# A two-attention decoder kernel: key copies shared by VectorE and ScalarE, later waits in TensorE's scores, and the first weights of the second attention on a semaphore of their own

## The reference, cut to what matters

```python
# layer 0, 16 heads of 32
q, k, v = split(x @ q_out), split(x @ k_out), split(x @ v_out)
w = softmax(where(causal, -inf, q @ k.T / sqrt(32)))
y = concat(w @ v) @ w_out
# layer 1, the same after a low-rank projection
...
cq  = layernorm(x @ W_dq)  * q_ln_g  + q_ln_b      # 512 -> 128
ckv = layernorm(x @ W_dkv) * kv_ln_g + kv_ln_b     # 512 -> 128
q = cq @ W_uq;  k, v = split(ckv @ W_ukv)
```

## Time and profile before

| what | value |
|---|---|
| time, median of 3 runs | 3426.01 us (3419.97 to 3428.82) |
| profiled execution: its own time | 3417.81 us |
| profiled execution: span | 3415.9 us |
| mean granted clock of TensorE | 0.954 |
| PE busy | 2988.1 us (87%) |
| DVE busy | 1672.7 us (49%) |
| ACT busy | 1237.4 us (36%) |
| POOL busy | 630.5 us (18%) |
| stage a0 | from the start to about 430 us |
| stage a1 | about 1722 to 2143 us |

### The profile page before, as it was taken

The page is one execution under the profiler, slowest core; times in us unless marked ns, Lnnn a source line. Parts: engine busy times, 40 slices in busy tenths (PEclk is TensorE's granted clock), DMA queues, the critical chain, the costliest instruction groups (busy, mean ns, idle before and its releaser), DMA issues. The chain is left out here.

```text
span 3415.9 us, 47727 instructions
## 1 busy us (share of the span) xinstructions
PE 2988.1 (87%) x16274; PEld 2012.9 (59%) x16274; DVE 1672.7 (49%) x3192; ACT 1237.4 (36%) x3212; POOL 630.5 (18%) x703
## 2 busy tenths in 40 slices
PE   6999958888883999999968888699999999899998
PEld 4676623333331777777734554588888888644443
DVE  5666657667771311111136666466666666311222
ACT  2324316655563211111124434455565555211111
POOL 1000031223222000000010002233333333110332
PEclk9999979988996999999989999899999999999999
DMA  1000056776554100000010011111121110522342
GB/s 62 25 25 12 19 128 139 148 151 127 124 134 127 61 13 13 13 13 13 7 47 25 25 37 56 50 44 50 50 75 62 50 49 26 188 63 85 109 170 74
DMA packets 128570, 229.67 MB, mean 67 GB/s; under 512 B 17061, under 2 KB 33765, under 8 KB 128400
## 3 DMA queue, kind: packets, MB, share of 16 engines
q1 hardware_dynamic: 98352, 174.73, 18.7%
q0 software_dynamic: 14096, 32.50, 3.1%
q10 hardware_dynamic: 15952, 20.15, 1.8%
HBM read 167.68 MB, written 61.00 MB: 67 GB/s over the span
## 5 line engine op out<-in xcount | busy, mean ns | idle before, releaser
L1393 DVE TENSOR_REDUCE x_minus_max<-banks 128x2 f32<-128x1024 f32 x256 | 308.1, 1223 | 156.3 <-PE banks L1459 154.6
L1341 ACT ACTIVATE x_probs<-banks 128x512 f32<-128x512 f32 x512 | 272.1, 598 | 140.3 <-PE banks L1477 131.6
L570 ACT ACTIVATE a_probs<-banks,a_minus_max 128x128 f32<-128x128 f32 (+1 forms) x512 | 209.1, 427 | 143.1 <-DVE a_minus_max L656 141.9
L2222 POOL TENSOR_TENSOR x_probs<-x_probs,x_inverse 128x512 f32<-128x512 f32 x128 | 133.3, 1042 | 266.5 <-DVE x_inverse L2428 266.5
L1477 PEld LDWEIGHTS banks<-x_stacked_q,x_stacked_k 53*128 53x128 f32 x512 | 62.1, 195 | 202.3 <-issue 155.0
L1477 PE MATMUL banks<-x_stacked_q,x_stacked_k 53*128 53x512 f32 x512 | 155.9, 514 | 27.6 <-ACT x_probs L1341 20.6
L2286 ACT ACTIVATE x_probs<-banks,x_minus_max,x_rroot 128x256 f32<-128x256 f32 x256 | 143.1, 567 | 87.9 <-DVE x_minus_max L2394 87.9
L3057 PE MATMUL banks<-m_w,m_xT 128*128 x368 | 169.0, 603 | 4.6 <-issue 4.6
L1459 PE MATMUL banks<-x_stacked_k,x_stacked_q 51*128 51x512 f32 x512 | 135.3, 478 | 42.7 <-DVE x_whole L1410 13.2
L656 DVE TENSOR_REDUCE a_minus_max<-banks 128x2 f32<-128x512 f32 (+1 forms) x192 | 131.7, 686 | 77.7 <-PE banks L810 59.7
L1809 DVE TENSOR_TENSOR f_hT<-banks,f_silu 128x256 f32<-128x256 f32 (+1 forms) x88 | 37.2, 424 | 265.6 <-ACT f_silu L1722 265.6
(11 more groups left out here) (385 smaller groups left out, 7739.6 us busy)
## 6 DMA issues: line engine op xcount, KB each, us to landing
x_parts_dram<-x_parts SPq DMA_DIRECT2D x16, 1024.0 KB, 6.0
x_x<-x_after SPq DMA_DIRECT2D x24, 512.0 KB, 4.2
x_stacked_k<-x_parts_dram SPq DMA_DIRECT2D x96, 128.0 KB
x_stacked_q<-x_parts_dram SPq DMA_DIRECT2D x96, 128.0 KB
x_after<-a_z SPq DMA_DIRECT2D x16, 512.0 KB, 2.7
x_z<-x_after SPq DMA_DIRECT2D x16, 512.0 KB, 6.6
x_heads_dram<-x_heads_out SPq DMA_DIRECT2D x32, 256.0 KB, 3.7
x_after<-x_z SPq DMA_DIRECT2D x16, 512.0 KB, 3.3
```

The costliest lines, as they stand in the source:

```text
L570: ins = act.activation(probs[:, n % 3, i * width:(i + 1) * width], psum[uses.bank(use)][:, i * width:(i + 1) * width], ACT.Exp, bias=minus ...
L1341: act.activation(probs[:, n % 8, :], psum[at.bank(f"exp{n}")], ACT.Exp, scale=SCALE)\
L1393: dve.tensor_reduce(minus_max[:, c % 2, h % 4:h % 4 + 2, t], at.pair(use), AX.X, ALU.max, negate=True)\
L2222: pool.tensor_tensor(probs[:, s % 4], probs[:, s % 4], inverse[:, s, :].unsqueeze(2).broadcast_to([P, TT, S1]), ALU.mult)\
```

## The change

Four edits, all in `self_attention`:

1. The four copies of k1 move from DVE's program to ACT's, behind q0 and q1 and ahead of v0 and v1. DVE keeps those of k0.
2. Ahead of S0, PE waits for q0, q1 and k0 alone. It waits for k1 ahead of S6, and for v0 and v1 ahead of the first `context`.
3. The two loads of w_down are issued by ACT, ahead of w_o, and count a new semaphore, `down_loaded`. PE waits for it ahead of the low-rank product.
4. PE's wait for the other small loads (six now) moves from its start to the head of each sequence.

```diff
-        SMALL = 8
+        down_loaded = sem("down_loaded")
+        SMALL = 6
 ...
         def _(pool):
             if latent:
-                pool.dma_start(w_down[:, :, 0:RANK], weights["dq"].rearrange("(c p) n -> p c n", p=P)).then_inc(weights_loaded, 16)
-                pool.dma_start(w_down[:, :, RANK:], weights["dkv"].rearrange("(c p) n -> p c n", p=P)).then_inc(weights_loaded, 16)
 ...
         def _(act):
+            if latent:
+                act.dma_start(w_down[:, :, 0:RANK], weights["dq"].rearrange("(c p) n -> p c n", p=P)).then_inc(down_loaded, 16)
+                act.dma_start(w_down[:, :, RANK:], weights["dkv"].rearrange("(c p) n -> p c n", p=P)).then_inc(down_loaded, 16)
 ...
+                act.wait_ge(k_cleared, 1)
+                use = f"k1.{u}"
+                wait_full(act, use, turn)
+                for i in range(4):
+                    rows = slice(DH * i, DH * i + DH)
+                    ins = act.copy(k_of_head[rows, 8 + i:8 + i + 5:4, :],
+                                   psum[uses.bank(use)][rows, :].rearrange("p (c t) -> p c t", c=2))
+                ins.then_inc(free[uses.bank(use)], 1)
                 for j in range(TT):
                     use = f"v{j}.{u}"
 ...
                 dve.wait_ge(k_cleared, 1)
-                for j in range(2):
-                    use = f"k{j}.{u}"
+                use = f"k0.{u}"
 ...
         def _(pe):
-            if latent:
-                pe.wait_ge(weights_loaded, 16 * SMALL)
 ...
             def low_product(turn, u, own):
+                pe.wait_ge(down_loaded, 32)
 ...
             def sequence(turn, u, following):
                 if latent:
                     wait_bank(pe, f"v1.{u}", turn)
+                    pe.wait_ge(weights_loaded, 16 * SMALL)
 ...
                     if n == 0:
-                        for w in ("q0", "q1", "k0", "k1", "v0", "v1"):
+                        for w in ("q0", "q1", "k0"):
                             wait_free(pe, f"{w}.{u}", turn)
+                    if n == 6:
+                        wait_free(pe, f"k1.{u}", turn)
 ...
+                    if c == 0:
+                        for w in ("v0", "v1"):
+                            wait_free(pe, f"{w}.{u}", turn)
```

More of the change, by code:

```diff
@@ L642, in sequence @@
                 dve.wait_ge(k_cleared, 1)
-                for j in range(2):
-                    use = f"k{j}.{u}"
[L645 to L650, removed]
+                use = f"k0.{u}"
+                wait_full(dve, use, turn)
+                for i in range(4):
+                    rows = slice(DH * i, DH * i + DH)
+                    ins = dve.tensor_copy(k_of_head[rows, i:i + 5:4, :],
+                                          psum[uses.bank(use)][rows, :].rearrange("p (c t) -> p c t", c=2))
+                ins.then_inc(free[uses.bank(use)], 1)
                 def row_max(n):
```

## The result

| | before | changed |
|---|---|---|
| median of the runs | 3425.28 us (3419.97 to 3428.82, 4 runs) | 3376.17 us (3368.01 to 3380.50, 4 runs) |
| profiled execution, its span | 3417.81, 3415.9 | 3374.49, 3372.7 |

The ratio is 0.9857, with a 95% interval of 0.984 to 0.9874: 49 us or 1.4% less. Forecast were 3381 us and 44.6 us less.

What follows compares the result with a forecast made beforehand. PE, 87% busy, was taken as the bound, so gains come from its idle or slow time: 7.3 + 22.5 + 8.5 + 6.3 = 44.6 us off the 3426.01 median gives 3381.4 us; range 3370 to 3400.

Steps and rivals of the forecast that it cites:

- The likeliest case: Whole kernel: all gains in a0 and a1 arrive, 44.6 us less, median 3381.4 us; chance 0.53.
- VectorE copies only k0: a1, ahead of S0: four fewer copies let S0 start 2.8 us earlier in each of eight sequences, 22.5 us.
- the clock: a1, S0 to S3: five slow sequences become fast with shorter idleness, 5 x 1.70 = 8.5 us; lower bound 0.
- The head: Start of a1: transposes start when x lands, not after the last small load; 6.3 us, or 2.2.
- ScalarE's copies: a1 and a0, four k1 copies at 0.48 us each on ScalarE: nothing waits, price 0.
- a0: a0, ahead of S0: the wait for v0 and v1 goes, 7.3 us over eight sequences; lower bound 6.1.
- The clock gives nothing: a1: the half clock moves to another stretch of the sequence, so 8.5 us are lost, 3390 us; chance 0.22.
- The head is held by DMA: Start of a1: x lands after 10.2 us, sharing engines with w_down; 4.1 us lost, 3385.5 us; chance 0.12.
- Copies dear: a1: ScalarE's copies take 1.4 us each, so a1's sequences gain only 10.4 us; 3402 us; chance 0.06.
- slower: a1: ScalarE's copies take 2.5 us each and delay the first exponential, 25 us lost; 3437 us; chance 0.03.
- Nothing in a1: a1: S0 meets another wait as late as the old; only a0 and head gain, 3412 us; chance 0.04.

Runs made afterwards that it cites:

- e1: Kernel before, with k1 copied by ScalarE ahead of v0 and v1, S0 still waiting for all six; 3412.86 us, ratio 0.997.
- e2: Kernel before, with only the shorter waits (S0 for q0, q1, k0); VectorE still copies both k; 3396.14 us, ratio 0.9932.
- e3: Kernel before, with only w_down on ScalarE's queue with its own semaphore and other small loads waited for later; 3416.66 us, ratio 0.9977.
- e9: Changed kernel, with k0 projected ahead of q0 and q1 in each sequence; 3364.27 us in one run.
- e6: Changed kernel, with four more ScalarE copies of k1 into an unread tile ahead of the bank's release; 3388.77 us, ratio 0.9896.
- e4: Changed kernel, with w_down issued by GpSimd ahead of the other small loads, still on its own semaphore; 3385.30 us, ratio 0.9896.
- e7: Kernel before, with k1 copied by ScalarE plus four unread copies, S0 still waiting for v1, now later; 3424.55 us in one run.
- e8: Changed kernel, with w_down laid out as 4 KB rows and loaded by one DMA; 3371.33 us in one run.
- e5: Changed kernel, with w_o issued only behind the first x^T copies, w_down left on ScalarE; 3380.77 us, ratio 0.9877.
- e10: Changed kernel, with both w_down in one 4 KB-row transfer and k0 projected first; 3368.47 us, ratio 0.9854.

## Why the prediction was right

**The sum, term by term.** The likeliest case came in, at 3376 against 3381. In a1 the profile gives 37.2 us, and the steps gave 22.5 + 8.5 + 6.3 = 37.3. The mechanism is the one forecast; that the numbers meet to 0.1 us is partly luck, since terms that were too large and too small cancel. Ahead of the first S0 a1 gained 10.3 us (39.1 to 28.8 behind the issue of x) where the steps had 9.1, and between the first and the last S0 27.2 where they had 28.2.

- *VectorE copies only k0, and the clock.* From the first S0 of a1 to the last it is 307.31 us, and was 334.46: 27.2 us less, where seven steps of 2.81 and five of 1.70 make 28.2. All eight S0 to S3 take 3.1 us. e1 and e2 are the two halves of the edit; each takes only part of the wait away, since k1's bank is written by S1. The last sequence gained 1.8 us and not 2.8; in the other kernels with this edit it is 48.1 to 48.9 us long, against 49.2 here and 51.0 before. What holds it is open.
- *The Trainium skill* ("TensorE: Matmul & The Clock Gate", HAM oscillation) says that pauses between groups of matmuls bring the half clock back each time. The doses agree in direction, but behind 2.9 to 3.5 us the clock fell in five and in six of eight sequences (before, e3), not in each, and the gain was the 8.5 us read from the rows, not 13.6.
- *The head.* The step took x as landing 6.0 us behind its issue and w_down as hidden. x landed after 4.8, so the transposes came 7.5 us earlier, but the second half of w_down took 7.9 us, and the product waited 1.70 for it: net 6.5 against 6.3. The prediction had 7.7 us for w_down in its hand and reached "hidden" only because it started the product from the later x. Two errors cancelled, and that is luck: with the same loads the product started 8.4 (e9), 9.3 (e3) and 12.2 us (e6) behind the issue of x, here 8.55. The early x is the change's own doing. In the five kernels where ScalarE issues w_o first (before, e1, e2, e4, e7) the first x lands after 6.0 to 6.1 us, in the seven where it issues w_down first after 4.6 to 4.8. Behind the product the first sequence gained 2.5 us at S0's wait (2.90 to 0.39) and 1.3 that no step had: its eight matmuls with w_ukv ahead of v took 1.89 us and not 3.18, at the higher clock. In e4 and e8 they took 3.02 and 2.90, so this part comes and goes.
- *ScalarE's copies.* The mis-sized term: 0.58 us each (four in 2.34), not 0.48. Copies of 128x512 in a pair gain by overlap (1.07 for two); these four do not. The price was still zero, because k1 is done at 1789.35 and the exponential is ready only at 1791.16. e6 shows where it stops being zero.
- *a0.* Measured 11.9 us, forecast 7.3. The first S0 came at 50.04 us and not 51.53, the last at 398.67 and not 410.46. Seven periods at 0.99 us (50.22 to 49.23 where neither has a surplus) make 6.9, which is the step's own part, and about 3 are two fewer stretches at the lower clock (five of seven periods had a surplus of about 1.4 us, now three). The edit is not shown to bring these: e1 and e7, where S0 waits in a0 as before, have two such periods, and e3 four; with the new waits it is one to three. The prediction had a0's clock only as a reason for the lower side of its range. The first S0 of a0 in the kernel before, and in the changed one, from their PE timelines:

```profile
51.53 1.10 PE L809 MATMUL banks<-a_k_of_head,a_qT 128*128 128x512 f32 x2 [0.72 <-issue]
```

```profile
50.04 1.02 PE L820 MATMUL banks<-a_k_of_head,a_qT 128*128 128x512 f32 x2
```

- *Outside these stages*, 6.4 us went back in x0 and f0, with a granted clock of 0.87 for 0.89. The change has no hand in it that any run shows. It was noise of this pair that offset a0's surplus.

**The rivals.** *The clock gives nothing* is refuted by the periods: from S0 to S0 it is 42.98 us and was 47.5, and of these 4.5 the earlier start is only 2.8. *The head is held by DMA*: half true. The product is held by a transfer, for 1.70 us, but x itself came early, so its 4.1 us were not lost. The Trainium skill ("DMA: Bandwidth & Descriptors", Issuing engines are not separate DMA queues) says that another issuer saves only the time of issuing. e4 agrees in the main: moving the issue from GpSimd to ScalarE is worth 1.2 us at the product, 0.8 of it in issuing. The transfers do share the way, as w_o's 11.7 and 5.1 us show. But w_down was not late by w_o: with w_o gone (e5) it took as long, and in one transfer of longer rows (e8) it landed after 4.2 us. *Copies dear* and *slower* needed 1.4 and 2.2 us a copy and met 0.58. *Nothing in a1* needed another wait as late as the old one: in e1 and e2 a shorter one of this kind exists, for v1 (1.86 us) and for k1's bank (1.63 us), which is why between the first and the last S0 either edit alone gives some 16 us and the changed kernel 27.2.

## What to carry to other kernels

Let the first consumer wait for what it reads, bank by bank, and look next at who writes the banks that are released later: here the shorter list of waits and the shorter queue of copies each moved the stall to another name, and only both removed it. A wait of a few microseconds that repeats ahead of matmuls may cost clock behind it too, which is to be read from the same instructions in two sequences, one slow and one fast. Where stages that an edit does not touch vary by 10 us and more, judge the edit by the duration of the stage that it does touch, and there by the rows that account for it.

## What the runs showed of the hardware that was not expected

- Of two loads of 256 KB in pieces of 512 B from ScalarE's queue the first landed 4.9 to 5.1 us behind its issue and the second after 7.8 to 11.5 (changed kernel, e3, e5, e6, e9); one load of 512 KB in rows of 4 KB landed after 4.2 and 4.1 us (e8, e10).
- Four 32x512 copies from PSUM on ScalarE take 2.34 us, four on VectorE 2.79; two 128x512 copies on ScalarE take 1.07. A quarter of the partitions makes a copy no shorter (0.58 us for 128x512 alone).
- With 2.9 to 3.5 us of idleness ahead of it, the same group of matmuls ran in part at half clock in five and six of eight sequences, with 1.9 to 2.1 in one and with 4.2 to 4.4 in all.
